# Cross-attention's K and V by Strassen's scheme over pairs of batches, K included

## The reference

```python
q = layernorm(x) @ Wq + bq
kv = context @ Wkv + bkv            # [32, 257, 1024]
k, v = jnp.split(kv, 2, axis=-1)    # 16 heads of 32
q, k = _larope(q, Lq), _larope(k, Lk)
scores = jnp.einsum('bhqd,bhkd->bhqk', q, k) * 64 ** -0.5
out = jnp.einsum('bhqk,bhkd->bhqd', softmax(scores), v)
x = x + out @ Wo + bo
```

## Time and profile before

| | |
|---|---|
| Time, median of 3 runs | 776.84 us (775.82 to 777.03) |
| The profiled execution: its time, its span | 779.38 us, 777.6 us |
| Mean granted clock of PE | 0.985 |
| Cross-attention | to 541.7 us of the span |
| Matmuls of 258 columns (K), three lines | 1,488 recorded, 423 us by duration |
| Largest groups on DVE / ACT / POOL | k_cos 51.0 / exp 63.5 / k_sin 93.4 us |

### The profile page before, as it was taken

One profiled execution on the slowest core, in us unless ns is written; L12 is line 12 of the kernel. 1 busy time (PEld: TensorE's weight loads), 2 busy tenths in 40 slices (PEclk: granted clock), 3 DMA queues, 4 the chain that ended last, 5 costly groups with the idle time before them and its releaser, 6 DMA issues. The chain is left out here.

```text
span 777.6 us, 23428 instructions
## 1 busy us (share of the span) xinstructions
PE 751.2 (97%) x9650; PEld 665.3 (86%) x9651; DVE 500.9 (64%) x1209; ACT 418.6 (54%) x978; POOL 336.6 (43%) x366
## 2 busy tenths in 40 slices
PE   8999999999999999999999999999899999599997
PEld 7899999999999999998999989997677777488784
DVE  6776765666575585675666557656889998622236
ACT  5465656556565566656656556664466664033330
POOL 1655456455454455544555445531133221246640
PEclk9989999999999999999999999999999999689999
DMA  8504010110011110011001100201942238634448
GB/s 294 208 29 164 27 40 29 36 57 30 29 36 36 49 37 29 32 33 57 30 29 49 44 30 29 83 29 57 408 174 110 105 122 350 207 114 166 162 140 319
DMA packets 23174, 77.96 MB, mean 100 GB/s; under 512 B 3328, under 2 KB 4736, under 8 KB 20128
## 3 DMA queue, kind: packets, MB, share of 16 engines
q1 hardware_dynamic: 19392, 64.45, 23.1%
q0 software_dynamic: 3680, 12.06, 4.7%
HBM read 57.89 MB, written 18.61 MB: 98 GB/s over the span
## 5 line engine op out<-in xcount | busy, mean ns | idle before, releaser
L164 PE MATMUL bank<-chi,wparts 128*128 128x258 f32 x496 | 143.2, 289 | 0.5 <-DVE v L759 0.5
L166 PE MATMUL bank<-chi,wparts 128*128 128x258 f32 x496 | 139.9, 282 | 0.0
L165 PE MATMUL bank<-clo,wparts 128*128 128x258 f32 x496 | 139.8, 282 | 0.0
L392 POOL TENSOR_TENSOR ksin<-kb,const 128x516 f32<-128x516 f32 x64 | 93.4, 1460 | 101.1 <-ACT kb L505 101.0
L505 ACT ACTIVATE kb<-bank,bias_cols 128x258 f32<-128x258 f32 x126 | 60.0, 476 | 66.4 <-PE bank L166 66.4
L412 POOL TENSOR_TENSOR ctx_sums<-craw 128x512 f32<-128x512 f32 x30 | 39.5, 1315 | 128.2 <-DVE ctx_sums_lo L776 128.2
L164 PEld LDWEIGHTS bank<-chi,wparts 128*128 128x128 f32 x496 | 93.8, 189 | 1.1 <-DVE v L759 0.7
L165 PEld LDWEIGHTS bank<-clo,wparts 128*128 128x128 f32 x496 | 94.1, 190 | 0.0
L166 PEld LDWEIGHTS bank<-chi,wparts 128*128 128x128 f32 x496 | 93.8, 189 | 0.0
L748 DVE TENSOR_TENSOR kcos<-kb,const 128x516 f32<-128x516 f32 x64 | 51.0, 798 | 29.6 <-ACT kb L505 29.6
L510 ACT ACTIVATE pr<-pr,nmax 128x257 f32<-128x257 f32 x128 | 63.5, 500 | 5.8 <-DVE nmax L784 5.8
(11 more groups left out here) (380 smaller groups left out, 2243.9 us busy)
## 6 DMA issues: line engine op xcount, KB each, us to landing
craw<-ctx_t_dram SPq DMA_DIRECT2D x32, 516.0 KB, 3.5
expert_lo<-weights_dram SPq DMA_DIRECT2D x8, 1024.0 KB, 12.5
expert_hi_scratch<-wraw SPq DMA_DIRECT2D x16, 512.0 KB, 2.7
wparts<-expert_hi_scratch SPq DMA_DIRECT2D x8, 1024.0 KB, 9.0
wraw<-weights_dram SPq DMA_DIRECT2D x7, 1024.0 KB, 5.8
expert_lo<-ffn_out_scratch SPq DMA_DIRECT2D x16, 256.0 KB, 5.8
x<-x_dram SPq DMA_DIRECT2D x8, 256.0 KB, 7.6
ffn_xn_scratch<-xn SPq DMA_DIRECT2D x8, 256.0 KB, 2.2
```

The lines of the kernel that those rows point to most:

```text
L164: pe.matmul(psum, ahi(c), bhi(c), start=(c == 0), stop=False)
L165: pe.matmul(psum, ahi(c), blo(c), start=False, stop=False)
L166: last = pe.matmul(psum, alo(c), bhi(c), start=False, stop=(c == chunks - 1))
L392: pool.tensor_tensor(ksin[:, part, :], kb[:, part, :], sink[:, part, :], ALU.mult).then_inc(s_ksin, 1)
```

## The change

K is now computed by the same seven-product scheme, and both K and V take two batches at once. For a pair q (batches 2q and 2q + 1, from q = 2) the two batches are the two block rows of the scheme, the halves of the 512 context features its two block columns; so the same four context differences (T1, T3, T2, T4, each 2 x 258 columns per partition) serve K and V. K takes two passes (c = 0, 1: which 128 columns of each half of W_K), each of seven products of six matmuls of 258 columns: 84 per pair in place of 96. V takes seven products of twelve matmuls of 256 columns: 84 per pair as before. Batches 0 to 3 are plain (before: V of 0 and 1), so batches 2 and 3 have 48 V matmuls each and no longer 42. The products add onto copies and sums:

```diff
-PLAIN = 2
+PLAIN = 4
...
+            K_PRODUCTS = ((0, 2), (0, 5), (0, 1), (0, 6), (0, 3), (0, 7), (1, 2), (1, 5), (0, 4), (1, 3), (1, 1), (1, 6),
+                          (1, 7), (1, 4))
+            K_COPIES = ((0, 5), (0, 1), (0, 6), (1, 5), (0, 4), (1, 1), (1, 6), (1, 4))
+            V_PRODUCTS = (2, 5, 1, 6, 3, 7, 4)
...
+                def ctx_sums_early(q):
...
+                    pool.tensor_tensor(t1_raw, craw[1][:, 0:2, :], craw[0][:, 0:2, :], ALU.subtract).then_inc(s_tr, 1)
+                    pool.wait_ge(s_tr, ctx_sum_of(q, R_T1))
+                    pool.tensor_tensor(craw[1][:, 0:2, :], craw[1][:, 2:4, :], craw[1][:, 0:2, :], ALU.subtract).then_inc(s_tr, 1)
+
+                def ctx_sums_late(q):
+
+                    pool.wait_ge(s_clo, parts_of(q, O_22))
+                    pool.wait_ge(s_tr, ctx_sum_of(q, R_T3))
+                    pool.tensor_tensor(craw[1][:, 2:4, :], craw[1][:, 2:4, :], t1_raw, ALU.subtract).then_inc(s_tr, 1)
+                    pool.wait_ge(s_tr, ctx_sum_of(q, R_T2))
+                    pool.tensor_tensor(craw[0][:, 2:4, :], craw[0][:, 2:4, :], craw[1][:, 2:4, :], ALU.subtract).then_inc(s_tr, 1)
...
+                        pe.wait_ge(s_clo, parts_of(q, {1: O_X1, 2: O_X1, 3: O_22, 4: O_T4, 5: O_T1, 6: O_T32, 7: O_T32}[k]))
...
+                def even_step(b, t, j):
+                    p, q = b // 2, b // 2 + 1
+                    more = q <= PAIR_LAST
+                    v_product(p, 6)
+                    v_product(p, 3)
+                    v_product(p, 7)
+                    probs_transposed(b)
+                    if more:
+                        k_product(q, 0, 2)
+                    else:
+                        self_product(0)
+                    v_product(p, 4)
+                    if more:
+                        k_product(q, 0, 5)
+                    extra_step(b, t, j)
+                    if more:
+                        k_product(q, 0, 1)
+                    diagonals_spread(b)
+                    attend(b, j)
+                    if more:
+                        k_product(q, 0, 6)
+
+                def odd_step(b, t, j):
+                    p = (b + 1) // 2
+                    k_product(p, 0, 3)
+                    k_product(p, 0, 7)
+                    k_product(p, 1, 2)
+                    k_product(p, 1, 5)
+                    probs_transposed(b)
+                    k_product(p, 0, 4)
+                    k_product(p, 1, 3)
+                    k_product(p, 1, 1)
+                    extra_step(b, t, j)
+                    k_product(p, 1, 6)
+                    v_product(p, 2)
+                    k_product(p, 1, 7)
+                    v_product(p, 5)
+                    k_product(p, 1, 4)
+                    diagonals_spread(b)
+                    attend(b, j)
+                    v_product(p, 1)
+
+                def last_step(b, j):
+                    self_product(1)
+                    probs_transposed(b)
+                    diagonals_spread(b)
+                    attend(b, j)
```

More of the change, by code:

```diff
@@ L350, in _ @@
[L350 to L365, removed]
@@ L447, in _ @@
                 pool.tensor_copy(same[:], const[:, C_SAME:C_SAME + P]).then_inc(s_same, 1)
[L448 to L462 removed]
+                k_sin_plain(0, 0)
@@ L477, in _ @@
-                body(0)
-                for t in range(1, TILES - 1):
-                    body(t)
-                body(TILES - 1, last=True)
+                        ln_and_bias(t, j)
+                        if b < B - 1:
+                            k_sin(b + 1, 2)
+                    else:
+                        for i in range(3):
+                            k_sin(b + 1, i)
+                        o_bias(b - 1)
+                        diagonals(b)
+                        if q <= PAIR_LAST:
+                            ctx_sums_late(q)
+                        ln_and_bias(t, j)
@@ L741, in q_rotate, with k_cos_plain @@
+                    dve.tensor_tensor(plain[:, :, 16:32], swap[:, :, 0:16], half(xn, odd), ALU.add)
+                    dve.tensor_tensor(swap[:, :, 0:16], swap[:, :, 0:16], half(xn, odd), ALU.add)
+                    dve.tensor_tensor(swap[:, :, 16:32], swap[:, :, 16:32], half(xn, even),
                                       ALU.subtract).then_inc(s_qr, 1)
-                def k_cos(b, half):
+                def k_cos_plain(b, half):
                     dve.wait_ge(s_kev, b * 4 + 2 * half + 2)
-                    if half == 0 and not at_start(b):
+                    if half == 0 and b > 0:
@@ L767, in v_12 @@
[L767 to L776 removed]
+                    dve.tensor_copy(v[b % 2][:, c, :], plain_v_bank(b, c)).then_inc(s_vd, 1)
@@ L1050, in plain_v_product @@
                         last.then_inc(s_vp1, 1)
-                def v_product(psum, rows, block, start):
-                    (hi, lo), (whi_i, wlo_i) = rows, wv_block(block)
-                    for c in range(2):
-                        pe.matmul(psum, hi[:, c, :], whi_i[:, c, :], start=start and c == 0, stop=False, skip_group_check=not start)
-                        pe.matmul(psum, hi[:, c, :], wlo_i[:, c, :], start=False, stop=False, skip_group_check=not start)
-                        last = pe.matmul(psum, lo[:, c, :], whi_i[:, c, :], start=False, stop=c == 1, skip_group_check=not start)
-                    return last
```

1121 lines of the change are left out of this document (692 added, 429 removed).

## The result

The changed kernel takes 830.33 us (827.24 to 831.04, 4 runs), the kernel before 776.93 us beside it (775.82 to 778.25). The ratio is 1.068, with an interval from 1.065 to 1.071: slower by 53 us, where 773.7 was forecast and 790 was the end of the range. The profiled execution took 831.04 us with a span of 829.2, against 779.38 and 777.6.

A forecast was written before the change was run, and what follows sets the result against it. PE, busy 97% of the span, was taken to bound the kernel. Saving -18.7, waits in seven tiles +10.1, end +4.5, start +1.0 sum to -3.1 us: 773.7 us from 776.84, with an 8-in-10 range of 762 to 790.

The forecast's parts named there:

- the even step: Cross-attention step laid out from its scores' start; PE reaches k(0,6) at T+13.9, waiting 0.5 us in j=0, 0.1 in j=2.
- the chain that I wrote down two sentences further on: Even step, DVE/POOL/ACT work up to the low part of T2 and T3: ready at 13.6 us, or 15.8 taking turns.
- The rival: Rival 3: PE's granted clock falls behind a wait in each of seven tiles, +24 us, 798 us; chance 0.05.
- The saving: Pairs 2 to 15: 168 fewer K matmuls, 20.2 us, less 1.4 for 12 more V matmuls; net 18.7 us.
- rival 4: PE's time per K matmul rises with shorter runs on one bank; 6 us of the gain go, 780 us; chance 0.04.
- Rival 1: DVE and POOL keep each other waiting in even steps; PE waits 1.9 us in j=0, 0.8 in j=2; 787 us; chance 0.31.
- My quarter of the way: PE's wait before k(0,6) in even steps, set between none and the full 1.9 us: 0.5 for j=0.
- The 8-column row: Profile row of the pair's low part on DVE, median 168 ns, read as DVE being held by POOL in few steps.
- 0.3 us for the copy of k(1,1): Odd step, j=1: k(1,6) waits for ACT's copy of k(1,1), 0.3 us lost.
- 0.17 for k(1,5): Odd step: PE waits before k(1,5) for DVE's first K sum behind four masked rows, 0.17 us, twice per tile.
- The ends: Late weight loads before self-attention: PE waits 3.7 us before the V product, AK's load and split add 0.8; together 4.5.
- 1.4 and 1.0: Start: 1.4 us for 12 more V matmuls in batches 2 and 3; 1.0 for split W_K sums and a reloaded weight.

The follow-up runs named there:

- the light run: Changed kernel, order kept; from pair 3 on k_cos, k_sin, the context's low parts and POOL's differences cover 8 of 258 columns: 784.42 us, ratio 1.010.
- the run with otlo early: Changed kernel with the low part of the output ahead of k_cos in DVE's order of the j = 0 steps: 795.25 us, ratio 1.025.
- the two best versions: Changed kernel with otlo early, k(0,1) copied before T4's high part, end reordered: 792.09 us; with T2 before the diagonals, k(0,1) copied before k(0,5): 792.11 us.

## Why the prediction was wrong

**The step that failed** is the even step: "PE reaches k(0,6) after scores 1.41, three V products 4.3, transposes 0.8, k(0,2) 0.7, v4 1.4, k(0,5) 0.7, the extra of 2.8 (the output or the q product)". The output product is in that line with its length alone, as if it had nothing to wait for. By the same line PE is there at 9.3 us; by the chain that I wrote down two sentences further on, DVE has block 22 at 9.3 and then k_cos, the statistics and o's low part, that is 12.0 at best and 14.6 in turn with POOL. Both numbers were in the text, and comparing them gives a wait of 2.7 to 5.3 us; the measured one is 4.7. The order excerpt for DVE showed `otlo` moving from first to behind them. I followed the chain to the last waiter and passed by an earlier one.

**The clock** was the second miss. The rival had 0.05, because "my waits are under 2 us"; with a wait of 4.7 the fall came in all seven tiles. The price given there, 24 us on top, was too high: the fall costs 13. Even this rival's 798 lies far below 830, since it had the fall without the wait in front of it.

**The saving** of 18.7 us counts the matmuls rightly (168 and 12, the difference in the instruction count is 156), and their pitch stayed 0.12. But the light run shows 1.7 us net per tile, not 2.9. This is near rival 4 in size, whose 6 us stand beside seven times 1.2, 8 us; its cause, a longer time for each K matmul, is not what the rows show: the time goes at the starts.

**Rival 1**, DVE and POOL in turn, was right in its mechanism and its place: with otlo out of the way, the wait stands before k(0,6), released by the low part of T3 and T2, 1.6 us at most against 1.9 expected. In the changed kernel it is hidden, because the output product's wait comes earlier in the same step and gives the chain those 4.7 us. My quarter of the way (0.5 us) was too little: in the even steps DVE and POOL hold each other up each time, not now and then, since k_cos, T2 and T4 were put side by side. The 8-column row, on whose median I leaned, says nothing about that; k_sin's median, 1.62 against 1.19, did.

**The small terms**: 0.3 us for the copy of k(1,1) and 0.17 for k(1,5) do not stand in the list of waits; 0.6 us between attend and k(0,6), for the copy of k(0,1), does, and I had none there, nor for the 0.3 to 0.6 us before k(1,7) in three odd steps, for the copy of k(1,6).

**The ends.** From batch 28 to the end of the phase there are 36 matmuls fewer than before, 4.3 us, and yet it takes 3.2 us longer: 7.5 us, where 4.5 was summed. The wait for AV's low part is 3.2 where 3.7 was summed, AK's 1.9 where 0.8 was, and behind the 3.2 the clock falls once more: the V product of self-attention takes 4.45 us instead of 2.91, which no term had. At the start, from batch 0 to batch 4, the run with otlo early takes 7.0 us more than the kernel before (71.3 against 64.3), where 1.4 and 1.0 were summed. Of these, 2.9 are 24 more matmuls, 12 of them in the plain V products of batches 2 and 3, the rest work of later batches that now comes earlier; 1.6 are the wait for otlo and 1.7 other small waits.

What stays open: the two best versions (792.09 and 792.11) are still 16 to 17 us above the kernel before, and no order of these calls tried here beats it. Whether a second buffer for the odd batch's K would was not tried. Why the clock fell behind some waits of 2.1 to 2.6 us and not behind others, the runs do not say.

## What to carry to other kernels

When a change puts PE's work in a new order, compare, at every wait of every engine in a step, when the waiter gets there and when its operand is ready, the untouched products too: one of these decided here, and moving one call took back 35 of 53 us. A saving of 2% on an engine that is 97% busy has to pay for each new chain through the other engines, and where these chains share buffers, and DVE and POOL hold each other up, removing one wait shows the next: four edges took turns here (otlo, the context's low part, the copy of k(0,1), the scores).

## What the runs showed of the hardware

- A wait of PE of 4.7 us brought the granted clock from 1.00 to 0.50 in all seven tiles, and in the one shown it came back some 7 us later; filling the wait with matmuls kept it up, worth 13 us. Waits of 2.6 to 2.8 us did so in four tiles and not in three others of the same execution, one of 2.07 us did, and with waits of 1.5 us the clock stayed at 1.00. The cost is thus not proportional to the wait.
- DVE and POOL operations that both read SBUF lengthened each other in both directions: three k_cos took 3.94 us beside three POOL operations and 1.83 us beside two short ones, otlo 1.30 us beside T2 for 0.28 of work, and POOL's second diagonals 1.07 us beside block 22's low part for 0.67.
- At a change between products and another kind of work one matmul took 0.20 to 0.23 us of PE instead of 0.12. The new order has 24 of these in a tile where the old one has 15, most of the 1.2 us of 62 that the order itself costs here.
